# The first group of an AdaLN feed-forward kernel: eight places for the split x, bias as a row through TensorE, splits in order of use

## What is computed

```python
# x (128, 32, 512); conv weight (32, 8, 9), 4 groups of channels; F = 1376
c   = conv1d(x, weight, padding=4, groups=4)               # 128 x 32 x 512
c   = c + (cond @ c_weight.T)[:, :, None] + bias[None, :, None]
g   = silu(c @ W_gate.T) * (c @ W_up.T)                    # over the last axis, 512 -> 1376
out = x + g @ W_down.T                                     # 1376 -> 512
```

## Time and profile before

| | |
|---|---|
| median of 3 runs | 781.6 us (780.97 to 782.45) |
| profiled execution, its time | 781.49 us |
| profiled execution, span | 779.7 us |
| mean granted clock of TensorE | 0.991 |
| TensorE products busy | 751.4 us, 96% |
| DVE, ACT, GpSimd busy | 432.9, 275.6, 103.8 us |
| DMA, mean rate | 195 GB/s |

### The profile page before, as it was taken

The page is one execution under the profiler, slowest core; times in us unless marked ns, Lnnn a source line. Parts: engine busy times, 40 slices in busy tenths (PEclk is TensorE's granted clock), DMA queues, the critical chain, the costliest instruction groups (busy, mean ns, idle before and its releaser), DMA issues.

```text
span 779.7 us, 10306 instructions
## 1 busy us (share of the span) xinstructions
PE 751.4 (96%) x3451; PEld 612.4 (79%) x3451; DVE 432.9 (56%) x707; ACT 275.6 (35%) x519; POOL 103.8 (13%) x131
## 2 busy tenths in 40 slices
PE   4749999999999999999999999999999999999998
PEld 4537888887888888887788888887788888887886
DVE  2578677676385555455753554555662444545224
ACT  2346555544352323323431333232442122333221
POOL 3534554620000110100100011100000000000000
PEclk9979999999999999999999999999999999999999
DMA  6265667657997767667542956766442776665402
GB/s 167 64 219 203 227 217 240 215 165 258 368 316 252 254 180 218 198 190 217 164 152 91 315 175 203 226 189 205 147 159 98 257 226 191 193 193 171 158 28 109
DMA packets 114260, 152.38 MB, mean 195 GB/s; under 512 B 11712, under 2 KB 49760, under 8 KB 114208
## 3 DMA queue, kind: packets, MB, share of 16 engines
q1 hardware_dynamic: 111904, 150.93, 60.9%
q10 hardware_dynamic: 2304, 0.79, 0.4%
HBM read 108.95 MB, written 34.34 MB: 184 GB/s over the span
## 4 chain that ended last, share of the span: by engine, by line
PE 94%; DVE 3%; DMA 1%; issue 0%; ACTq 0%; ACT 0%; SPq 0%; DVEq 0%
PE bank L657 54%; PE bank L689 31%; PE bank L577 3%; PE bank L572 3%; PE bank L552 2%; DMA x_in<-in_x 1%; DVE hc_lo L946 1%; PE bank L613 1%; PE bank L595 0%; PE bank L586 0%; DVE xt_lo L946 0%; DVE g_all L1041 0%; ACTq L869 0%; DVE g_all L1144 0%; DVE ring L946 0%
## 5 line engine op out<-in xcount | busy, mean ns | idle before, releaser
L657 PE MATMUL bank<-hc_hi,ring 128*128 128x512 f32 (+1 forms) x1232 | 386.7, 395 | 9.9 <-DVE hc_lo L946 9.8
L657 PEld LDWEIGHTS bank<-hc_hi,ring 128*128 128x128 f32 (+1 forms) x1232 | 225.7, 186 | 60.6 <-issue 6.4
L657 PE MATMUL bank<-hc_lo,ring 128*128 128x512 f32 (+1 forms) x616 | 241.5, 392 | 0.0
L689 PE MATMUL bank<-ring,g_hi 128*128 128x512 f32 (+1 forms) x704 | 218.6, 392 | 0.0
L689 PEld LDWEIGHTS bank<-ring,g_hi 128*128 128x128 f32 (+1 forms) x704 | 131.2, 188 | 28.1 <-DVE g_lo L946 0.8
L748 ACT ACTIVATE mix<-bank 128x512 f32<-128x512 f32 (+1 forms) x132 | 78.9, 597 | 209.6 <-PE bank L657 209.6
L689 PE MATMUL bank<-ring,g_lo 128*128 128x512 f32 (+1 forms) x352 | 137.2, 390 | 0.0
L657 PEld LDWEIGHTS bank<-hc_lo,ring 128*128 128x128 f32 (+1 forms) x616 | 114.6, 186 | 26.9
L946 DVE TENSOR_TENSOR g_lo<-g_all,g_hi 128x512 fp32r<-128x512 f32 (+1 forms) x88 | 60.9, 694 | 83.8 <-ACT g_hi L748 83.8
L748 ACT ACTIVATE g_hi<-g_all 128x512 fp32r<-128x512 f32 (+1 forms) x88 | 55.1, 629 | 114.1 <-PE bank L689 114.1
L1110 DVE TENSOR_TENSOR mix<-bank,mix 128x512 f32<-128x512 f32 (+1 forms) x44 | 30.4, 691 | 94.0 <-ACT mix L851 94.0
(11 more groups left out here) (101 smaller groups left out, 541.1 us busy)
## 6 DMA issues: line engine op xcount, KB each, us to landing
ring<-saved SPq DMA_DIRECT2D x319, 256.0 KB, 2.9
saved<-ring SPq DMA_DIRECT2D x99, 256.0 KB, 2.6
g_all<-in_x SPq DMA_DIRECT2D x32, 256.0 KB, 3.6
out_y<-g_all SPq DMA_DIRECT2D x32, 256.0 KB, 3.4
x_in<-in_x SPq DMA_DIRECT2D x13, 512.0 KB, 5.1
stage<-win SPq DMA_DIRECT2D x96, 64.0 KB, 2.3
w_nat<-in_L_ffn_W_gate SPq DMA_DIRECT2D x10, 256.0 KB, 3.5
w_nat<-in_L_ffn_W_up SPq DMA_DIRECT2D x10, 256.0 KB, 3.5
```

The lines of the kernel that those rows point to most:

```text
L657: mm = pe.matmul(bank[0:w, :], wt, hv, start=fresh and q == 0 and t == 0, stop=q == 1 and t == 2, skip_group_check=not fresh)
L689: mm = pe.matmul(acc(half, tt)[:], gs, wd, start=f == 0 and t == 0, stop=f == FC - 1 and t == 2)
```

## The change

Only group 0 is touched.
- *Places.* The split x of group 0 goes into eight places instead of two: the tail of `hc_hi` and `hc_lo` (kinds `K_S1` and on), free until the convolution is done. `split_x` of group 0 no longer waits for `conv_done`, nor repeats a first block of 128 columns; `split_h` of the kinds that lie there waits for `conv_done`.
- *Order in the convolution.* `split_x(0, k + 2)` comes ahead of `read_conv(0, k)`, `turn_x(0, k + 3)` ahead of `conv_step(0, k)`. `turn_gate(0)`, `turn_up(0)`, `prepare(0, ·)` come one step earlier, and `prepare` on DVE ahead of the reading. The `RAW_A1` splits move into steps 6 and 7, on DVE q = 0 ahead of `read_conv(0, 7)`.
- *Setup.* The convolution weights are split before the context weights are spread; the Toeplitz products come first; ACT reads one of their two banks and DVE the other; the context products come after two turned blocks of x, in other banks (`up_ps`). GpSimd's block of k = 1 no longer waits for ACT's block of k = 0, which has a semaphore of its own.
- *Bias.* Instead of four DMAs of a column to all partitions and an addition on DVE, one DMA brings a row of 32, GpSimd repeats it, and TensorE adds it with four further products (the row against ones); ACT copies the sum out.
- *Splits after the convolution.* They come in the order in which the products use them and the chunks land; `prepare(1, 0)` comes ahead of the splits of `RAW_B2` and `K_S4`.

```diff
+        xt_first = [part[:, K_S1:, :, :].rearrange("p k q t -> p (k q t)") for part in (hc_hi, hc_lo)]
 # GpSimd
-                elif k == 1:
-                    pool.wait_ge(x_blocked, 1)
-                else:
+                elif k > 1:
                     pool.wait_ge(x_turned, k - 1)
+            pool.wait_ge(bias_loaded, LD)
+            pool.tensor_copy(bias_rep..., bias_row...broadcast_to([1, G, R, CG])).then_inc(consts, 1)
             block_x(0, 1)
 # TensorE
-                    mm = pe.matmul(conv_ps[:, g * P:(g + 1) * P], ctx_w_rep[:, g, :, :], cond_t, start=True, stop=True)
+                    pe.matmul(up_ps[:, at], ctx_w_rep[:, g, :, :], cond_t, start=True, stop=False)
+                    mm = pe.matmul(up_ps[:, at], bias_rep[:, g, :], ones, start=False, stop=True)
             setup_transposes()
+            toep_products()
+            turn_x(0, 0)
+            turn_x(0, 1)
             ctx_products()
-            turn_x(0, 0)
-            toep_products()
-            turn_x(0, 1)
+            turn_x(0, 2)
+            conv_head(0)
             for k in range(STEPS):
-                if k == 0:
-                    conv_head(0)
-                if k + 2 < STEPS:
-                    turn_x(0, k + 2)
+                if k + 3 < STEPS:
+                    turn_x(0, k + 3)
+                if k == 2:
+                    turn_gate(0)
                 if k == 3:
-                    turn_gate(0)
-                if k == 4:
                     turn_up(0)
                 conv_step(0, k)
 # ACT
             def split_x(grp, k):
-                if k >= 2:
-                    act.wait_ge(conv_done, CPG * grp + k)
-                elif grp > 0:
-                    act.wait_ge(conv_done, CPG * grp)
+                if grp > 0:
+                    act.wait_ge(conv_done, CPG * grp + (k if k >= 2 else 0))
...
+            act.wait_ge(toep_mm, 1)
+            hi(toep[:, :, 0:QN // 2, :], setup_a...).then_inc(toep_done, 1)
+            split_toep(0)
             split_x(0, 0)
-            split_toep(0)
+            split_x(0, 1)
+            act.wait_ge(ctx_mm, 1)
+            hi(ctxb[:], up_ps[:].rearrange("p (g n) -> p g n", g=G)).then_inc(ctx_done, 1)
             for k in range(STEPS):
-                if k < STEPS - 1:
-                    split_x(0, k + 1)
-                if 3 <= k <= 6:
-                    prepare(0, k - 3)
+                if k + 2 < STEPS:
+                    split_x(0, k + 2)
+                if 2 <= k <= 5:
+                    prepare(0, k - 2)
                 if k in (4, 6):
                     stage_second(k // 2 - 1)
-            split_h(0, RAW_A1, 0)
-            split_h(0, RAW_A1, 1)
+                if k >= 6:
+                    split_h(0, RAW_A1, k - 6)
             stage_second(3)
+            for kind in (RAW_A2, K_S1, K_S2):
+                split_h(0, kind, 0)
             split_h(0, K_S3, 0)
             split_h(0, K_S3, 1)
             copy_chain(0, 0, 0)
-            for kind in (RAW_A2, K_S1, K_S2, RAW_B2, K_S4):
+            for kind in (RAW_A2, K_S1, K_S2):
+                split_h(0, kind, 1)
+            prepare(1, 0)
+            for kind in (RAW_B2, K_S4):
                 split_h(0, kind, 0)
-            for kind in (RAW_A2, K_S1, K_S2, RAW_B2, K_S4):
                 split_h(0, kind, 1)
 # DVE
+            split_conv_w()
             copy_ctx_w()
-            split_conv_w()
+            read_toep()
+            split_toep(0)
             split_x(0, 0)
-            read_toep()
-            read_ctx()
-            split_toep(0)
+            split_x(0, 1)
+            read_head(0)
             for k in range(STEPS):
-                if k < STEPS - 1:
-                    split_x(0, k + 1)
-                if k == 0:
-                    read_head(0)
+                if k + 2 < STEPS:
+                    split_x(0, k + 2)
+                if 2 <= k <= 4:
+                    prepare(0, k - 2)
                 read_conv(0, k)
-                if 3 <= k <= 5:
-                    prepare(0, k - 3)
...
+                if k >= 6:
+                    split_h(0, RAW_A1, k - 6)
+            mix_h_first(K_S1, 0)
+            mix_h_first(K_S2, 0)
+            for kind in (RAW_A2, K_S1, K_S2):
+                split_h(0, kind, 0)
+            split_h(0, K_S3, 0)
+            split_h(0, K_S3, 1)
+            split_h(0, RAW_A2, 1)
+            mix_h_first(K_S1, 1)
+            mix_h_first(K_S2, 1)
+            split_h(0, K_S1, 1)
+            split_h(0, K_S2, 1)
+            prepare(1, 0)
+            mix_h_first(K_S4, 0)
+            mix_h_first(K_S4, 1)
+            for kind in (RAW_B2, K_S4):
+                split_h(0, kind, 0)
+                split_h(0, kind, 1)
```

More of the change, by code:

```diff
@@ L540, in turn_x @@
             def turn_x(grp, k):
-                pe.wait_ge(x_blocked, STEPS * grp + k + 1)
+                if grp == 0 and k == 0:
+                    pe.wait_ge(x_blocked_first, 1)
+                else:
+                    pe.wait_ge(x_blocked, STEPS * grp + k)
                 if grp == 0 and k == 0:
@@ L591, in turn_up @@
                 pe.wait_ge(permuted[1], f + 1)
+                if f == 0:
+                    pe.wait_ge(ctx_done, 1)
                 if f > 0:
@@ L825, in split_h @@
                     act.wait_ge(product_done[kind], FC * g)
+                elif kind >= K_S1:
+                    act.wait_ge(conv_done, CPG)
                 hi(dst, src).then_inc(hc_hi_done[kind], 1)
@@ L907, in _ @@
                     last = f == FC - 1
-                    if more:
+                    if more and f > 0:
                         prepare(f + 1, 0)
@@ L957, in split_conv_w @@
                     if n < 2:
-                        last.then_inc(parts, 1)
-                        dve.wait_ge(parts, 2 * n + 1)
-                        dve.tensor_tensor(conv_w_rest[:, n, :], rest, conv_w_t[:, n, :], ALU.subtract).then_inc(parts, 1)
-                        dve.wait_ge(parts, 2 * n + 2)
+                        last.then_inc(setup_t, 1)
+                        dve.wait_ge(setup_t, 2 * n + 2)
+                        dve.tensor_tensor(conv_w_rest[:, n, :], rest, conv_w_t[:, n, :], ALU.subtract).then_inc(setup_t, 1)
+                        dve.wait_ge(setup_t, 2 * n + 3)
                 last.then_inc(conv_w_ready, 1)
-            def read_ctx():
-                dve.wait_ge(ctx_mm, 1)
-                dve.wait_ge(bias_loaded, LD * G)
-                dve.tensor_tensor(ctxb[:], conv_ps[:].rearrange("p (g n) -> p g n", g=G),
-                                  bias_col[:].broadcast_to([P, G, P]), ALU.add).then_inc(ctx_done, 1)
             def read_toep():
                 dve.wait_ge(toep_mm, 1)
-                for n, bank in enumerate((setup_a, setup_b)):
-                    q0 = n * (QN // 2)
-                    last = dve.tensor_copy(toep[:, :, q0:q0 + QN // 2, :],
-                                           bank[:, 0:QN // 2 * CH].rearrange("p (q g o) -> p g q o", g=G, o=CG))
-                last.then_inc(toep_done, 1)
+                q0 = QN // 2
+                dve.tensor_copy(toep[:, :, q0:QN, :], setup_b[:, 0:q0 * CH].rearrange("p (q g o) -> p g q o", g=G, o=CG)
+                                ).then_inc(toep_done, 1)
             def split_toep(grp):
                 if grp == 0:
-                    dve.wait_ge(toep_done, 1)
+                    dve.wait_ge(toep_done, 2)
                 dve.wait_ge(t_hi_done, grp + 1)
@@ L988, in split_x @@
                 dve.wait_ge(xt_hi_done, STEPS * grp + k + 1)
-                at = (k % 2) * WB * P
-                last = lo(xt_lo[:, at:at + WB * P], xt_bank(grp, k)[:], xt_hi[:, at:at + WB * P])
-                if k % 2 == 0 and k > 0:
+                at = xt_at(grp, k)
+                last = lo(xt(grp)[1][:, at:at + WB * P], xt_bank(grp, k)[:], xt(grp)[0][:, at:at + WB * P])
+                if grp > 0 and k % 2 == 0 and k > 0:
                     last = lo(xt_lo[:, 2 * WB * P:], xt_bank(grp, k)[:, 0:P], xt_hi[:, 2 * WB * P:])
```

83 lines of the change are left out of this document (39 added, 44 removed).

## The result

The changed kernel takes 774.23 us in the median of 4 runs (771.86 to 775.86), the kernel before 781.29 beside it: a ratio of 0.9903, 95% interval 0.9886 to 0.9921, 7.1 us faster by the medians and 7.6 by the ratio. Forecast were 775.3 and 6.3 us. The profiled execution is the quickest of the four, 771.86 us.

A forecast was written before the change was run, and what follows sets the result against it. TensorE idles 28.3 us, some 25 ahead of 62 us, so the start of the `RAW_B2` product decides; DVE limits after the convolution. Gains 1.6 + 4.05 + 0.65 = 6.3 us from 781.6 give 775.3, range 772.4 to 778.3.

The forecast's parts named there:

- The frame: Whole kernel: 28.3 us of TensorE idle time can be won, some 25 of it ahead of 62 us.
- The setup, to 19.6 with a gain of 1.6: Start to the reading of step 0: readable at 19.6 us against 21.20 before, gain 1.6.
- The convolution, 17.3 for 21.36: Convolution loop, 19.6 to the last reading's end at 36.9: 17.3 us for 21.36, gain 4.05.
- DVE low part 0.4: Convolution loop, `prepare` ahead of the reading: DVE's low part after ACT's raw halves takes 0.4 us.
- A1's low part behind the issues: Convolution end: DVE's A1 split before `read_conv` 7 waits for ACT's high part behind DMA issues, costing 2.4 us.
- After the convolution, 22.35: From the last reading (36.9) to the `RAW_B2` product (59.27): 0.65 us of the gain lies here.
- GpSimd's meetings: After the convolution: GpSimd's copies beside DVE's list cost 2.5 us, with bounds of nothing and 5.18.
- The clock stayed low through the setup: Rival, setup: low clock throughout loses 2 us, total 777.3; chance 0.24 together with GpSimd shutting DVE out in full.
- The lock-out in full: Rival, after the convolution: GpSimd shuts DVE out fully, gain 3.6, total 778.0; chance 0.24 together with the low setup clock.
- the low clock in the eight steps: Rival, convolution: low level through all eight steps, 3.4 us each, ending at 46.5, total 784.9; chance 0.05.
- a wait behind 66 us: Rival, behind 66 us: storing and refilling of weights swallows the 6 us, total 781.6; chance 0.04.
- `gate_a` much before 54: Sign of being wrong, after the convolution: `gate_a` much before 54 us or after 57; 54.7 was forecast.

The follow-up runs named there:

- the first profile: Profile of the changed kernel from its first timing against the kernel before: the profiled run took 771.86 us, median 774.23 us.
- the second profile: The changed kernel timed again unaltered, beside the kernel before: median 774.99 us, ratio 0.9900; the profiled run took 775.35 us.
- the grouped form: Changed kernel with the four bias row products behind the four context products instead of between them, part of the context lost: 771.21 us, ratio 0.9873.
- the last kernel: Changed kernel with A1's high part earlier, its low parts later, GpSimd's f = 2 weights first, bias products grouped, one start flag: 768.09 us, ratio 0.9826.
- two moved lines: Changed kernel with DVE's A1 low parts behind the last reading (771.14 us, 0.9863), or with ACT's A1 high part ahead of its DMA issues (771.14 us, 0.9871).
- the exchanged copies: Changed kernel with GpSimd's reordering of the f = 2 weights ahead of its block of group 1's x: 773.81 us, ratio 0.9899.
- the combined kernel: Changed kernel with both A1 moves, GpSimd's f = 2 weights first and bias products grouped: 767.85 us with four start flags, 768.09 with one.

## Why the prediction was right, and where not

- *The frame* held: all of the gain lies ahead of `RAW_B2`, 714.0 us follow in either kernel, and no wait appeared behind it.
- *The setup, to 19.6 with a gain of 1.6*, is the step that failed, twice. The forecast let the loads be where they were ("x at 10.2") and put the four DMAs of the column at nothing, without a reason: they held x back by 4.1 us, 5.1 us of the run. And from x to the reading it counted 9.4 us, with context products of 0.52 us and a rise of the clock at 16.5 after "work without a pause": alternating with products of one row they take 0.72, and the clock stayed down through all eight (13.3 us from x to the reading), or had risen and fell behind them (10.9). So the forecast of 19.6 was off by −4.1 and +1.5 us in the first profile (17.01), and by −3.6 and +3.9 in the second (19.89), where the errors cancel. With the column's DMAs back the new setup reads step 0 at 22.6, 1.4 us later than the old one, not 1.6 earlier, though x is there sooner. What the new order won (2.4 us from x to the reading), the bias products took once (2.3) or twice (4.7).
- *The convolution, 17.3 for 21.36*, mechanism right, measured 18.1. The mis-sized term is "DVE low part 0.4" of `prepare(0, 0)`: the two took 1.59 us, beside GpSimd's copy at 20.68, where two such parts take 0.76 without a copy (49.91 above). The sum had left GpSimd out in this loop; counted from the reading of step 0, they end 0.9 us later than forecast. The order of waits was as told, up to A1's low part behind the issues: 2.4 forecast, 2.4 and 1.9 measured by taking it away at either end.
- *After the convolution, 22.35*, measured 21.0 to 21.1. The last low parts ended earlier, at 16.6 us behind the convolution instead of 17.8; DVE started A2 q = 1 0.5 us sooner, since ACT's high parts follow each other at 0.55, not 0.62; and `gate_a` to `RAW_B2` took 4.4 for 4.57. GpSimd's meetings, put at 2.5, cost that: the sum at 43.14 took 1.40 us instead of 0.69, and the rows at 44.46 and 46.55 took 2.17 and 1.64 instead of 1.29 and 0.76, 2.5 us in all. The upper bound of 5.18 was not approached.
- *The rivals.* The clock stayed low through the setup in the second profile, as one of them had it; that profile reads step 0 2.9 us later than the first, 2.4 of it without the later x (2 forecast). The lock-out in full didn't come, nor did the low clock in the eight steps, nor a wait behind 66 us. Eight slow steps of 3.4 us behind 19.6 would have ended at 46.8 and not at 46.5 as that rival's sum has it; nothing hangs on it.
- *Luck.* The median of 774.2 against 775.3 is close because x came earlier than assumed and the context and bias products took longer. The forecast of the total had the right size; its account of the setup was wrong. One of its own signs of being wrong, `gate_a` much before 54, is there in the first profile (51.7), though not in the second (54.8).

What stays open: what decides in which run the clock is up during the context and bias products. In the two profiles of the changed kernel x lands within 0.5 us of the same time, and TensorE idles for 0.3 us ahead of block 0 in the second only; but the grouped form and the last kernel differ in their level without any such difference.

## What to carry to other kernels

Look at what a removed DMA did to its neighbours, not only at its own wait: four DMAs that spread a column to 128 partitions in pieces of four bytes made the load of x land 4 us later. Ask of every operation that is moved ahead of a reading which other queue it waits for; here a 0.7 us split put a wait for another engine's DMA issues (2.8 us) onto the path, and either of two moved lines won 2 to 3 us. A gain measured alone need not survive beside others: the 1.1 us of the exchanged copies was gone in the combined kernel. And when a sum comes out right, compare its terms: here two errors of 3.6 and 3.9 us stood against each other.

## What the hardware showed unasked

- Four products of 1 row by 128 columns, between four of 128 rows, cost as much as these: 0.72 us each at the low level when alternating, 0.42 at the high one; 0.46 and 0.50 at the low level when each kind stood together, and 0.28 for the row products at the high one.
- TensorE was busy from 5.6 us on in the second profile but for 0.3 us, and its clock rose only near 19 us; without the row products it was up for the first step's products at 12.9 us (0.23 apart) in a profile whose TensorE had stood for 0.9 us shortly before. In the grouped form and the last kernel the same rows up to 11.07 us were followed by a clock that was up at once in one and rose near 18.5 us in the other. Busy time alone does not tell when it rises.
- A DMA of 0.5 KB in four-byte pieces took 3.0 to 8.1 us to land (four of them, kernel before), and the four delayed what was issued beside them on another queue: 64 KB by 2.4 us, 512 KB by 4.0.
